# The o gate of an LSTM step gets a bank, a tanh and semaphores of its own

## The reference, cut to what matters

```python
def step(carry, xs):
    h, c = carry
    xi_t, xf_t, xg_t, xo_t = xs
    i_t = jax.nn.sigmoid(xi_t + h @ V_i)
    g_t = jnp.tanh(xg_t + h @ V_c)
    o_t = jax.nn.sigmoid(xo_t + h @ V_o)
    c_new = h * c + i_t * g_t
    h_new = o_t * jnp.tanh(c_new)
    return ((h_new, c_new), h_new)
(_, _), hs = lax.scan(step, (h0, c0), (xi, xf, xg, xo))
```

## Time and profile before

| what | value |
|---|---|
| median of 3 runs | 3993.85 us |
| lowest and highest | 3993.41, 3995.58 us |
| the profiled execution, its own time | 3996.03 us |
| span of its trace, first to last instruction | 3994.3 us |
| PE busy | 3584.6 us, 90% |
| DVE busy | 3374.4 us, 84% |
| ACT busy | 2527.2 us, 63% |
| POOL busy | 2156.5 us, 54% |
| first and last gates' tanh | 196.8 and 3989.0 us |

### The profile page before, as it was taken

How to read it: one execution, slowest core, us unless ns; L and a number is a source line. 1 busy time by engine, 2 the same in 40 slices (tenths; PEclk the granted TensorE clock), 3 DMA queues, 4 the chain that set the end, 5 groups by cost and what they waited for, 6 DMA issues and landing times.

```text
span 3994.3 us, 130407 instructions
## 1 busy us (share of the span) xinstructions
PE 3584.6 (90%) x35548; PEld 2659.6 (67%) x35548; DVE 3374.4 (84%) x21816; ACT 2527.2 (63%) x11668; POOL 2156.5 (54%) x3179
## 2 busy tenths in 40 slices
PE   6899999989899999999999999999989899988888
PEld 5666666666666666666666666666666666666665
DVE  6688888888888888888888888888888888888887
ACT  4366666666666666666666666666666666666565
POOL 6655565656565656555555555565655565652222
PEclk7955555555555555555555555555555555555555
DMA  5000000000000000000000000000000000000000
GB/s 74 2 1 1 1 1 1 1 1 1 1 1 1 1 1 1 1 1 1 1 1 1 1 1 1 1 1 1 1 1 1 1 1 1 1 2 1 1 1 1
DMA packets 44538, 11.06 MB, mean 3 GB/s; under 512 B 39914, under 2 KB 44011, under 8 KB 44491
## 3 DMA queue, kind: packets, MB, share of 16 engines
q1 hardware_dynamic: 42378, 10.05, 1.6%
q10 hardware_dynamic: 2112, 0.46, 0.1%
HBM read 7.29 MB, written 3.21 MB: 3 GB/s over the span
## 4 chain that ended last, share of the span: by engine, by line
PE 66%; DVE 14%; ACT 13%; issue 5%; POOL 1%; DMA 0%; DVEq 0%; ACTq 0%; POOLq 0%
PE GATES L1343 14%; PE YB L1163 10%; PE GATES L1413 9%; ACT O L747 7%; PE H1B L1157 7%; ACT G L743 6%; DVE O L998 6%; PE YB L1314 6%; PE TAPB L1150 6%; PE DB L1282 5%; DVE HR L1002 5%; PE DB L1144 3%; PE H2B L1190 1%; PE H1B L1190 1%; PE H2B L1138 1%
## 5 line engine op out<-in xcount | busy, mean ns | idle before, releaser
L743 ACT ACTIVATE G<-GATES 128x12 f32<-128x12 f32 x3136 | 571.1, 182 | 1206.8 <-PE GATES L1413 1195.2
L1413 PEld LDWEIGHTS GATES<-HR,VW 128*128 128x128 f16 x6272 | 421.4, 107 | 601.5 <-issue 556.7
L1343 PE MATMUL GATES<-HR,VW 128*128 128x4 f16 x3136 | 531.8, 170 | 306.9 <-DVE HR L1002 214.0
L989 DVE TENSOR_TENSOR_SCAN CT<-G,CT 128x12 f32<-128x12 f32 x3136 | 586.5, 187 | 247.8 <-ACT G L743 218.7
L747 ACT ACTIVATE O<-G 128x8 f32<-128x8 f32 x3136 | 663.2, 211 | 98.7 <-ACT G L743 0.2
L998 DVE RECIPROCAL O<-O 128x4 f32<-128x4 f32 x3136 | 568.3, 181 | 175.1 <-ACT O L747 0.3
L1409 PEld LDWEIGHTS <-VW 128*128 128x128 f16 x3136 | 457.3, 146 | 354.3 <-issue 317.7
L976 DVE SCALAR_TENSOR_TENSOR CT<-HIST,CT 128x4 f32<-128x4 f32 x3136 | 522.0, 166 | 126.9 <-DVE HIST L1008 13.1
L1413 PE MATMUL GATES<-H,VB 128*128 128x4 f16 x6272 | 619.3, 169 | 0.0
L1413 PE MATMUL GATES<-HR,VW 128*128 128x4 f16 x6272 | 614.5, 168 | 0.0
L1163 PE MATMUL YB<-HD,W 128*64 128x112 f32 x3840 | 596.0, 412 | 1.7 <-DVE HD L869 1.7
(11 more groups left out here) (245 smaller groups left out, 6993.2 us busy)
## 6 DMA issues: line engine op xcount, KB each, us to landing
out_dram<-OUT SPq DMA_DIRECT2D x112, 28.0 KB, 1.9
X<-in_x_dram SPq DMA_DIRECT2D x4, 672.0 KB, 10.9
STG<-in_L_ffn_w_dram SPq DMA_DIRECT2D x4, 512.0 KB, 12.7
U<-in_L_conv_U2s_dram SPq DMA_DIRECT2D x1, 972.0 KB
W<-in_L_ffn_w_dram SPq DMA_DIRECT2D x1, 512.0 KB, 12.0
X<-in_x_dram ACTq DMA_DIRECT2D x4, 112.0 KB, 3.2
S<-in_L_conv_S1s_dram SPq DMA_DIRECT2D x1, 108.0 KB
S<-in_L_conv_S2s_dram SPq DMA_DIRECT2D x1, 108.0 KB
```

The source lines that it names most:

```text
L743: act.activation(G6[:, :, 2:5], gates[c][:, w, :, :], ACT.Tanh, scale=1 / GSCALE).then_inc(step_in, 1)
L989: dve.tensor_tensor_scan(CELL.rearrange("z b k -> z (b k)"), G6[:, :, :].rearrange("z b k -> z (b k)")[:, 0::2], ADD3.rearrange("z b k -> ...
L1343: return pe.add_instruction(mybir.InstMatmult(name=nc.get_next_instruction_name(), engine=mybir.EngineType.PE, start_tensor_calc=False, st ...
L1413: last = pe.matmul(gates[c][:, w, :, SLOT[g]], wt[:, g].rearrange("z m c -> z (m c)"), digit, start=False, stop=True, skip_group_check=True)
```

## The change

The o gate moves out of the GATES banks into the bank DB, 112 columns for each half row. GATES keeps c and i. A step's matmuls stand in the same order, but the second of the VB three now raises gates_done, and the third raises a new count, gate_o_done. ACT's first tanh takes c and i alone (8 elements), a second tanh takes o from the bank DB into OT, four columns in that same bank, and 1 + o is made from OT behind its own count, ot_done. The tanh of c and i also waits for h_done, the history of the step in front.

Since DB now holds o, the token's weights go into H1B during the recurrence (weights_bank), and the spread normalisation factors into H2B (spread). With that the next first layer, and the duplication at column 54, wait for DBS and not for SI. The first H2 of a row waits for the copy of those factors (RSC). ACT zeroes the half of DB that is next to be filled, at columns 1 and 49, behind o1_done, and the o matmul at columns 2 and 50 waits for that. The o inputs are filled in at column 5 and at column 54, behind o1_done of the same column.

```diff
-        PRE0={51: (0, 1, 2), 52: (3, 4), 53: (5, 6), 54: (7, 8)}, COPY=None, RSE=None)
+        PRE0={51: (0, 1), 52: (2, 3), 53: (4, 5)}, PRE0_O={54: (6, 7, 8)}, COPY=None, RSE=None)
...
-PRE1_AT = {3: (0, 1, 2, 3, 4), 6: (5, 6, 7, 8)}
-SLOT = (2, 0, 1)
+INPUTS = (("b", 0), ("b", 1), (0, 0), (0, 1), (1, 0), (1, 1), ("b", 2), (0, 2), (1, 2))
+FIRST_O = INPUTS.index(("b", 2))
+PRE1_AT = {3: (0, 1, 2, 3, 4, 5), 5: (6, 7, 8)}
+ZERO_AT = (1, 49)
+SLOT = (1, 0)
...
-        gates = [g[:, 0:HALF * B * 3].rearrange("z (k b t) -> z t b k", b=B, k=3) for g in GATES]
+        gates = [g[:, 0:HALF * B * 2].rearrange("z (k b t) -> z t b k", b=B, k=2) for g in GATES]
+        GATE_O = [DB[:, c * TOK:(c + 1) * TOK] for c in range(2)]
+        gate_o = [g.rearrange("z (b t) -> z t b", b=B) for g in GATE_O]
+        OT = DB[:, 448:448 + B]
...
+                    act.wait_ge(h_done, 1 + n)
                     act.wait_ge(gates_done, 1 + n + 1)
-                    act.activation(G6[:, :, 2:5], gates[c][:, w, :, :], ACT.Tanh, scale=1 / GSCALE).then_inc(step_in, 1)
+                    act.activation(G6[:, :, 2:5:2], gates[c][:, w, :, :], ACT.Tanh, scale=1 / GSCALE).then_inc(step_in, 1)
+                    act.wait_ge(gate_o_done, 1 + n + 1)
+                    act.activation(OT[:, :], gate_o[c][:, w, :], ACT.Tanh, scale=1 / GSCALE).then_inc(ot_done, 1)
                     act_registers(act, j, t, involution)
-                    act.wait_ge(step_in, 1 + 2 * n + 2)
-                    act.activation(O5[:, :, 1:5:3], G6[:, :, 3:4].broadcast_to([128, B, 2]), ACT.Copy, scale=O_MAX, bias=1.0)\
-                        .then_inc(o1_done, 1)
+                    act.wait_ge(ot_done, 1 + n + 1)
+                    act.activation(O5[:, :, 1:5:3], OT[:, :].unsqueeze(2).broadcast_to([128, B, 2]), ACT.Copy, scale=O_MAX,
+                                   bias=1.0).then_inc(o1_done, 1)
...
+                    for k in range(2):
+                        if t == ZERO_AT[k]:
+                            act.wait_ge(o1_done, 1 + n + 1)
+                            act.activation(GATE_O[1 - k], CST[:, CZERO:CZERO + 1].broadcast_to([128, TOK]), ACT.Copy).then_inc(oz_done, 1)
...
-                pe.wait_ge(si_done, 1 + NG * j + k)
+                if lstm:
+                    pe.wait_ge(dbs_done, 1 + NG * j + k)
...
-                        for g in range(1, 3):
-                            last = pe.matmul(gates[c][:, w, :, SLOT[g]], wt[:, g].rearrange("z m c -> z (m c)"), digit,
-                                             start=False, stop=True, skip_group_check=True)
-                    last.then_inc(gates_done, 1)
+                        last = pe.matmul(gates[c][:, w, :, SLOT[1]], wt[:, 1].rearrange("z m c -> z (m c)"), digit,
+                                         start=False, stop=True, skip_group_check=True)
+                        if wt is VB:
+                            last.then_inc(gates_done, 1)
+                        if wt is VW and t - 1 in ZERO_AT:
+                            pe.wait_ge(oz_done, 1 + 2 * (j - LAG) + ZERO_AT.index(t - 1) + 1)
+                        last = pe.matmul(gate_o[c][:, w, :], wt[:, 2].rearrange("z m c -> z (m c)"), digit,
+                                         start=False, stop=True, skip_group_check=True)
+                    last.then_inc(gate_o_done, 1)
```

More of the change, by code:

```diff
@@ L81, in head_places @@
         GAT=0, IXF=0, DM=((0, 0), (0, 0)), DT=(1, 1), DP=2, DPLO=3, DUPX=50, X4=51, DUP=53, XS=54, OUT3=54, OUT2=54,
-        PRE0={55: tuple(range(9))}, COPY=5, RSE=23)
+        PRE0={55: tuple(range(9))}, PRE0_O={}, COPY=5, RSE=23)
 OUT_FREE_AT = (13, 48)
-PRODUCTS = 3 + 2 * 3
-PRE1_AT = {3: (0, 1, 2, 3, 4), 6: (5, 6, 7, 8)}
-SLOT = (2, 0, 1)
+INPUTS = (("b", 0), ("b", 1), (0, 0), (0, 1), (1, 0), (1, 1), ("b", 2), (0, 2), (1, 2))
+PRODUCTS = len(INPUTS)
+FIRST_O = INPUTS.index(("b", 2))
+PRE1_AT = {3: (0, 1, 2, 3, 4, 5), 5: (6, 7, 8)}
+ZERO_AT = (1, 49)
+SLOT = (1, 0)
 MAIN, HEAD = main_places(), head_places()
@@ L241, in spread, with weights_bank @@
         def spread(lstm):
-            return DB if lstm else GATES[1]
+            return H2B if lstm else GATES[1]
+        def weights_bank(lstm):
+            return H1B if lstm else DB
         def logits(lstm):
@@ L278, in build_program @@
             "conv_done slot3_done slot2_done res4a_done res4_done")
-        (dupx_done, x4_done, pre0_done, pre1_done, gates_done, step_in, o1_done, cell_done,
+        (dupx_done, x4_done, pre0_done, pre1_done, gates_done, gate_o_done, oz_done, step_in, ot_done, o1_done, cell_done,
          t_done, rec_done, hd1_done, hd2_done, h_done, ocopy_done, oadd_done, ostored) = lstm_sems = sems(
-            "dupx_done x4_done pre0_done pre1_done gates_done step_in o1_done cell_done "
+            "dupx_done x4_done pre0_done pre1_done gates_done gate_o_done oz_done step_in ot_done o1_done cell_done "
             "t_done rec_done hd1_done hd2_done h_done ocopy_done oadd_done ostored")
@@ L702, in act_fill @@
                 act.wait_ge(hd_done, 1 + NG * j + k)
-                act.activation(DBS[:, :], DB[:, 0:EG * 2 * TOK], ACT.Copy).then_inc(dbs_done, 1)
+                act.activation(DBS[:, :], weights_bank(lstm)[:, 0:EG * 2 * TOK], ACT.Copy).then_inc(dbs_done, 1)
         def act_registers(act, j, t, involution):
@@ L1122, in _, with prefill @@
                 dve_row(dve, j, first, before, False, True, True, True)
[L1126 to L1131, removed]
+        def prefill(pe, c, k, lstm):
+            d, g = INPUTS[k]
+            bank = GATE_O[c] if g == 2 else GATES[c][:, SLOT[g] * TOK:(SLOT[g] + 1) * TOK]
+            if d == "b":
+                return pe.matmul(bank, BX[:, g].rearrange("z m c -> z (m c)"), ONEH[:, :],
+                                 start=(k == 0 or (k == FIRST_O and not lstm)), stop=False, skip_group_check=True)
             xs = X4S[:, :].rearrange("z (p q w) -> z p q w", p=2, q=Q)[:, :, :, c * HALF:(c + 1) * HALF]
-            return pe.matmul(GATES[c][:, SLOT[g] * TOK:(SLOT[g] + 1) * TOK].rearrange("z (q p t) -> z p q t", q=Q, p=2),
+            return pe.matmul(bank.rearrange("z (q p t) -> z p q t", q=Q, p=2),
                              UX[:, d, g].rearrange("z m c -> z (m c)"), xs, start=False, stop=False, skip_group_check=True)
@@ L1251, in pe_fill @@
                         pe.wait_ge(step_in, 1 + 2 * (j - LAG) * W)
-                    last = prefill(pe, 1, k)
+                    if k == FIRST_O:
+                        pe.wait_ge(o1_done, 1 + (j - LAG) * W + t + 1)
+                    last = prefill(pe, 1, k, lstm)
                     if k == PRODUCTS - 1:
@@ L1281, in pe_fill @@
                     for p in range(2):
-                        last = pe.matmul(DB[:, (2 * m + p) * TOK:(2 * m + p + 1) * TOK], SEL[:, p, EG * k + m, :], DP[:, :],
+                        last = pe.matmul(weights_bank(lstm)[:, (2 * m + p) * TOK:(2 * m + p + 1) * TOK], SEL[:, p, EG * k + m, :], DP[:, :],
                                          start=(m == 0 and p == 0), stop=True, skip_group_check=True)
@@ L1288, in pe_fill @@
                         pe.wait_ge(x4_done, 1 + j + 1)
-                    last = prefill(pe, 0, k)
+                    last = prefill(pe, 0, k, lstm)
                     if k == PRODUCTS - 1:
@@ L1327, in pe_fill @@
             if t == P.DUP:
-                if experts:
+                if experts and lstm:
+                    pe.wait_ge(dbs_done, 1 + NG * (j + 1))
+                elif experts:
                     pe.wait_ge(si_done, 1 + NG * (j + 1))
@@ L1339, in pe_fill @@
                     duplicate(pe, GATES[0], XD4).then_inc(dupx_done, 1)
+                for k in P.PRE0_O.get(t, ()):
+                    if k == FIRST_O:
+                        pe.wait_ge(o1_done, 1 + (j - LAG) * W + t + 1)
+                    last = prefill(pe, 0, k, lstm)
+                    if k == PRODUCTS - 1:
+                        last.then_inc(pre0_done, 1)
         def multiply_loaded(pe, out, weights, moving):
@@ L1350, in pe_registers @@
             P = MAIN
+            if t - 1 in ZERO_AT:
+                pe.to_reg(1 + 2 * (j - LAG) + ZERO_AT.index(t - 1) + 1)
             if t == P.MEAN[0]:
@@ L1372, in pe_registers @@
                 pe.to_reg(1 + 2 * (j - LAG) * W)
+            if FIRST_O in PRE1_AT.get(t, ()) or FIRST_O in P.PRE0_O.get(t, ()):
+                pe.to_reg(1 + (j - LAG) * W + t + 1)
             if t in P.PRE0 and 0 in P.PRE0[t]:
```

15 lines of the change are left out of this document (7 added, 8 removed).

## The result

The changed kernel takes 4117.5 us (median of 4 runs, 4117.2 to 4120.4) against 3994.5 us for the kernel before (4 runs, 3993.4 to 3995.6). The ratio is 1.031, with a 95% interval of 1.030 to 1.032: **123 us slower**, where 98 us faster was forecast. The profiled execution took 4120.4 us, its span is 4118.6 us.

The account below looks back on a forecast made before the run. Hand-overs between engines along the cell's path were taken to bound each step, 1206 ns summed. 3136 steps x 32 ns = 100.4, less 2.0, gave 98 us off: 3896 us, range 3880 to 3965, the forecast's own 3880 to 3915.

Parts of the forecast that it names:

- the part on waits and moved fill: New waits, zeroing and moved fills around the recurrence: h_done's wait over early, the rest paid out of pauses; cost 0.
- the 32 ns of gain: Per step on the cell's path: 29 from the earlier matmul count and 3 from the shorter tanh.
- the path of o: Tanh of o, 1 + o, reciprocal, to H5: H5 free at 690 ns, 11 before the cell's path needs it.
- (b): Rival at the o tanh: ACT starts it behind the first tanh, at 179 not 73; 198 us slower, 4192; chance 0.07.
- (c): Rival at DVE's fills of 224 columns: they bind the scan, 43 us less gain, 3939 us; chance 0.06.
- (d): Rival at the VB matmuls: the second's count arrives no earlier than the third's; only 3 ns left, 3986 us; chance 0.03.
- The cell's path: Tanh of c and i, scan, cell's tanh, HR, H5, VB matmuls to the next tanh: 1174 ns a step.
- (a): Rival on the o path: it ends last in part, 1 + o keeping 211 ns; 44 us less gain, 3950; chance 0.12.
- Where the gain is not had: Columns 8 and 9 in the recurrence: 1.6 us and 0.4 us of the gain lost, others none.

Follow-up runs that it names:

- e1_swap: The changed kernel with the two waits in front of the tanh of c and i in the other order, gates_done first, h_done second: 3947.0 us, ratio 0.988.
- e2_before_wait: The kernel before with a wait for h_done added in front of the gates_done wait at the gates' tanh: 4175.5 us, ratio 1.046.
- e5_before_second: The kernel before with a wait for h_done added behind the gates_done wait at the gates' tanh: 3997.1 us, ratio 1.001.
- e3_sixth: e1_swap with the tanh of c and i waiting for the sixth matmul's count and not the fifth's: 4044.6 us, ratio 1.013.
- e4_no_tanh_o: e1_swap without the tanh of o, 1 + o made straight from the o gate's sum: 3924.2 us, ratio 0.982.
- e8_dve_wait: The kernel before with a second, long-met wait (o1_done) named first in front of HR on DVE: 4287.5 us, ratio 1.074.
- e9_relu96: e1_swap with column 0's waits in the changed kernel's order, plus the second Relu (REDF) on 96 partitions, not the last 32: 3938.3 us, ratio 0.986.

## Why the prediction was wrong

**The step that failed** is in the part on waits and moved fill: "The wait for h_done is over early", and so 0. The count is early, as said. But the prediction asked only when the new wait is over, and not what a second wait does to the first. It takes gates_done off the tanh and puts it on an instruction in front, and the tanh then starts 60 ns later than if it had waited itself, in 3080 of 3136 steps: 60 x 3080 = 185 us. e1_swap and e2_before_wait show it as 170 us from one side and 181 from the other, and e5_before_second that the wait is free in the other order. Of the 32 ns of gain 20 were left after the path of o and the small terms, and the wait took three times that. The list of the changed kernel had shown the hint, two waits on the tanh of c and i where there was one. In the recurrence of before such pairs stand only in the fills. In front of DBS both waits are long met; there the activation follows the cell's tanh by 0.08, and that row was taken for the cost of a wait. It says nothing of a wait that ends last.

The price of such a wait could have been read from the trace of before, in the rows that run ahead of the recurrence. The silu of line 698 waits there for two counts. The one named second, of VV on DVE, ends last, and ACT is idle until then:

```profile
L697 ACTq EVENT_SEMAPHORE  x1: 17/17/17, 158.8 to 158.8; - x1
```

```profile
158.86 0.54 ACT L698 ACTIVATE SI<-H1B 128x448 f32<-128x448 f32 x1 [2.13 <-DVE VV L844]
```

It starts 62 ns after its semaphore instruction, and so it does at 115.1, 132.9 and 185.9 us. On DVE, between lines 854 and 855, the same is 65 to 69 ns in 17 such places.

**None of the rivals was it.** (b) had the right sign and the wrong cause. The o tanh starts 74 ns behind the first, as taken from the rows, and not at 179. An estimate by the figures of the Trainium skill (ScalarE: Activation LUTs, section What ACT_TABLE_LOAD costs) would put that start at 100 ns and the length of the tanh of o at 189; the trace has 74 and 172, so the slower time here is no support for that rule. (c) and (d) fall too: the scan starts 213 to 216 ns after the tanh also behind the fills of 224 columns, and the fifth matmul's count is early, worth 31 ns a step (e3_sixth).

**The cell's path** was right to 4 ns. Without the tanh of o the period is 1178, against 1174 summed; the gates' tanh fell to 181 and not 179. The gain by the count was 29 and measured 31, some 6 of them from the slower hand-over behind the sixth matmul.

**The path of o** was summed to end 11 ns before the cell's and ends about with it. The term that was mis-sized is the o tanh: 159 forecast and 172 measured when it follows directly on another (158 at column 6, where it doesn't). 1 + o was good, 182 against 180. So the reciprocal ends at 671 and not 658, and by it H5 is free at 703, which is 2 ns before the cell's path lets it start (705 in e4_no_tanh_o). H5's scan takes 195 and not 188 in every run that has the tanh of o; that this comes from the reciprocal's count, which is there only just before, is argued and not shown. The period is 1187 in e1_swap, 13 more than summed, 9 by the path of o and 4 by the cell's; in the changed kernel 12, since 1246 less 60 is 1186, which is 38 us. (a) was partly right in what it costs, though 1 + o did not keep its 211.

**Where the gain is not had** was right for column 8 (1262 to 1267, before 1260 to 1266). Column 9 took nothing that shows. The five columns with the convolution (19 to 39) were left out: they stood at 1214 in the kernel before and gained only 7 ns in e1_swap. Column 6 was not foreseen: 1367 against 1246, 50 x 121 = 6 us; the kernel before already has 1220 there.

The sum again, from what was measured: 3896, + 184 for the wait, + 39 for the path of o and the tanh, + 5 for column 6 (13 of its 121 are in the forecast), - 6 for the columns whose own delays are hidden by the longer step (8, 9 and the five with the convolution): 4118.

The working was uneven as well. Each operation of the loop was bounded by rows, down to a few ns; of the waits in the diff it was only asked whether they are met.

## What to carry to other kernels

In a loop that is bound by the hand-overs between engines, count the waits of each instruction on it. Where there are two on ACT or DVE (the other engines weren't tried), name first the one that ends last, so that it stays on the instruction itself, and read from the order or the trace which of them became a semaphore instruction; where the first wait hangs on a register operation, as at a loop's start here, it is the other way round. The place to look is the hand-over: here 205 ns from a matmul's start to the tanh, against some 266 with the semaphore instruction between. And where a change adds a second wait to the loop, look in the trace of before for any operation, also outside the loop, that such an instruction let go from idle: its row has the price.

## What the runs showed of the hardware

- An ACT operation let go by a semaphore instruction starts 62 ns after that one's start, which is 60 more than a wait on the operation itself costs. On DVE it is 66 after, and 71 more (HR at 700 and not 629 after the gates' tanh, e8_dve_wait). The Trainium skill (Perfetto Trace Analysis, section Identifying Dependency Chains) says that such instructions may be inserted, and its section Per-engine timelines has an operation decoded and pushed into a wait queue, where it waits for its semaphores. The trace agrees with the first: 3080 of them. The 62 ns would then be that decoding and pushing, which a wait on the operation hides; no run here shows them apart.
- Two activations that read PSUM and write 8 and then 4 elements start 74 ns apart, though the first takes 181. The second then takes 172, and 158 where it starts after the first's end (column 6).
- An activation with scale and bias tensors on partitions 64 to 95 doesn't start beside the one in front: 0.19 us behind it and not 0.08. The second tanh after it is late as well. With partitions 0 to 95 neither happens (e9_relu96). The copies on 32 partitions from 0 at column 10 (DP, without such tensors) do start at once, so the number of partitions alone isn't the cause; whether the start at 64 alone is, or only with the tensors, wasn't tried. How far it reaches isn't known either: in the same rows the copy NMX at column 24 starts 186 ns behind the cell's tanh in the changed kernel, and 74 in e9_relu96 and in the kernel before, which has REDF on 32 partitions too. DP in the changed kernel:

```profile
1608.51 0.16 ACT L765 ACTIVATE CT<-CT 128x8 f32<-128x8 f32 x1
1608.58 0.24 ACT L699 ACTIVATE DP<-TAPB 32x112 f16<-32x112 f32 x1
```
